# Keys of a cross-attention: one product of 128 rows per half and copies by transfers, in place of eight products of 96 rows

## What is computed

```python
x = x + xattn(layernorm(x), ctx, mask, Wq, Wk, Wv, Wo)
x = x + ffn(layernorm(x), gate_w, wi_gate, wi_up, wo)
# xattn
q = shape(H @ Wq, Lq) * dph ** (-0.5)
k = shape(T @ Wk, Lkv)
v = shape(T @ Wv, Lkv)
scores = jnp.einsum('bhqd,bhkd->bhqk', q, k) + ext      # ext: finfo.min where mask is 0
out = jnp.einsum('bhqk,bhkd->bhqd', softmax(scores), v) @ Wo
# ffn: top 2 of 8 experts for each token, a capacity for each expert and rank,
# silu(disp @ wi_gate) * (disp @ wi_up) @ wo, weighted and added back
```

## Time and profile before

| what | us |
|---|---|
| median of 3 runs (385.32 to 386.65) | 385.34 |
| the profiled execution, its own time | 385.02 |
| its span in the trace | 383.2 |
| TensorE busy, share of the span | 348.0, 91% |
| VectorE / ScalarE / GpSimd busy | 251.2 / 193.4 / 228.4 |
| last row scores of the attention's pair 14, 15 begin | 128.0 |
| first slots loaded for the experts | 170.5 |

### The profile page before, as it was taken

One profiled execution on the slowest core, in us unless ns is written; L12 is line 12 of the kernel. 1 busy time (PEld: TensorE's weight loads), 2 busy tenths in 40 slices (PEclk: granted clock), 3 DMA queues, 4 the chain that ended last, 5 costly groups with the idle time before them and its releaser, 6 DMA issues.

```text
span 383.2 us, 8985 instructions
## 1 busy us (share of the span) xinstructions
PE 348.0 (91%) x3013; PEld 304.9 (80%) x3013; DVE 251.2 (66%) x933; ACT 193.4 (50%) x439; POOL 228.4 (60%) x195
## 2 busy tenths in 40 slices
PE   5899799999999996668999999999999999999970
PEld 2566577687778764558999999999999999999970
DVE  5898999999999996604455554645546455465440
ACT  3578677787888873303344444434434343344320
POOL 6373512667667777740464573864848638368673
PEclk9899999999999998598999999999999999999995
DMA  6899301222323222124137245463373544724232
GB/s 179 244 359 297 92 7 23 63 67 67 82 55 118 72 66 68 53 60 124 15 30 168 33 42 162 37 150 54 37 173 34 114 82 38 176 21 38 28 34 21
DMA packets 41159, 34.33 MB, mean 90 GB/s; under 512 B 8337, under 2 KB 37521, under 8 KB 40977
## 3 DMA queue, kind: packets, MB, share of 16 engines
q1 hardware_dynamic: 26592, 23.67, 21.0%
q0 software_dynamic: 13568, 9.58, 18.2%
q10 hardware_dynamic: 960, 0.60, 0.6%
HBM read 21.12 MB, written 17.73 MB: 101 GB/s over the span
## 4 chain that ended last, share of the span: by engine, by line
PE 68%; DVE 14%; POOL 6%; issue 4%; ACT 3%; DMA 3%; SPq 1%; POOLq 1%; DVEq 0%; ACTq 0%
PE bank L921 18%; PE bank L676 11%; PE bank L678 10%; PE bank L677 10%; PE bank L779 5%; POOL slots L441 4%; DVE mneg L1027 4%; PE bank L747 3%; PE bank L770 2%; PE bank L912 2%; DVE rall L1077 1%; PE bank L797 1%; DMA maskr<-in_mask 1%; PE bank L730 1%; PE bank L731 1%
## 5 line engine op out<-in xcount | busy, mean ns | idle before, releaser
L475 POOL DMA_INDIRECT out<-ys,idx x80 | 125.0, 1562 | 83.8 <-DVE ys L1308 52.1
L1335 DVE TENSOR_TENSOR h<-sg,bank 128x256 f32<-128x256 f32 x160 | 66.2, 419 | 86.8 <-ACT sg L661 78.7
L661 ACT ACTIVATE sg<-bank 128x256 f32<-128x256 f32 x160 | 61.5, 385 | 107.7 <-PE bank L678 107.2
L676 PE MATMUL bank<-ex_hi,w_hi 128*128 128x256 f32 x320 | 95.8, 299 | 1.0 <-DVE ex_lo L1289 0.3
L678 PE MATMUL bank<-ex_lo,w_hi 128*128 128x256 f32 x320 | 89.5, 280 | 0.0
L677 PE MATMUL bank<-ex_hi,w_lo 128*128 128x256 f32 x320 | 89.5, 280 | 0.0
L921 PE MATMUL bank<-w_raw,h 128*128 128x128 f32 x640 | 78.0, 275 | 0.8 <-DVE h L1335 0.8
L921 PEld LDWEIGHTS bank<-w_raw,h 128*128 128x128 f32 x640 | 74.9, 192 | 0.9 <-DVE h L1335 0.9
L441 POOL DMA_INDIRECT slots<-rall,slot x64 | 62.7, 980 | 18.4 <-issue 17.5
L676 PEld LDWEIGHTS bank<-ex_hi,w_hi 128*128 128x128 f32 x320 | 60.9, 190 | 4.1 <-issue 2.5
L677 PEld LDWEIGHTS bank<-ex_hi,w_lo 128*128 128x128 f32 x320 | 61.0, 190 | 0.0
(11 more groups left out here) (122 smaller groups left out, 536.7 us busy)
## 6 DMA issues: line engine op xcount, KB each, us to landing
slots<-in_empty SPq DMA_DIRECT2D x8, 660.0 KB, 10.7
xl<-slots SPq DMA_DIRECT2D x7, 660.0 KB, 7.3
w_raw<-in_wgu SPq DMA_DIRECT2D x8, 512.0 KB, 3.7
w_raw<-in_wdn SPq DMA_DIRECT2D x8, 256.0 KB, 4.3
out<-X SPq DMA_DIRECT2D x16, 128.0 KB
X<-in_x SPq DMA_DIRECT2D x3, 512.0 KB, 5.5
out<-ys,idx POOLq DMA_INDIRECT x80, 3.3
slots<-rall,slot POOLq DMA_INDIRECT x64
```

Of the source, the lines that this page charges most:

```text
L475: nc.gpsimd.indirect_dma_start(out=out[:, :], out_offset=bass.IndirectOffsetOnAxis(ap=IDX[v][:, j:j + 1], axis=0), in_=YS[c][:, t, :], in_ ...
L661: nc.scalar.activation(SG[m % 2][:], GATE_PS[m % 2][:, 0:2 * P], ACT.Silu).then_inc(sg_ready, 1)
L676: nc.tensor.matmul(ps, hi, m_hi, start=True, stop=False)
L1335: nc.vector.tensor_tensor(H[n % 2][:, f, :], SG[m % 2][:], UP_PS[m % 2][:, 0:2 * P], ALU.mult).then_inc(h_ready, 1)
```

## The change

- `project_keys(half)`: one product of three parts with all 128 output rows for each half of the batches; the host orders Wk's columns so that output row 4c+g is feature c of group g. Half 0 is made in the front, half 1 in step 1.
- `keys_hi(half)` writes the high part over the masked context `CTXM`, `keys_lo(half)` the low part over `CTX_LO`.
- `arrange_keys(piece)` on SyncE's queue: three transfers copy hi, hi and lo into `KC`, whose layout becomes group, batch, key. Pieces are batches 0 to 1, 2 to 7 (both issued ahead of the X loads) and 8 to 15 (issued after the expert weights' loads).
- `place_keys(j)`: one transfer for each batch, 32 in place of 16 for each j.
- `mask_context(1)`, `context_hi(1)`, `context_lo(1)` move from the front into step 0.
- The mask row is formed after `context_lo(0)` and `moments(0)`.
- TensorE's front: `project_values(0)` stands before the turning of the first batch.

```diff
-PLACED = 16 * 4 * HG
+PLACED = 16 * 4 * HG * 2
-        KC = s1("kc", [P, B, GROUPS, LK])
+        KC = s1("kc", [P, GROUPS, B, LK])
-        K_PS = [MX[0], MX[1], DEN_PS, M1, M1, M1, M1, M1]
+        K_PS = M1
@@ block.sync
             for g in range(GROUPS):
-                sp.dma_start(KC[ONE_ROW:ONE_ROW + 1, :, g, :], EXT[:]).then_inc(ext_in, 16)
+                sp.dma_start(KC[ONE_ROW:ONE_ROW + 1, g, :, :], EXT[:]).then_inc(ext_in, 16)
+
+            def arrange_keys(piece):
+
+                b0, b1 = ((0, 2), (2, 8), (8, 16))[piece]
+                sp.wait_ge(k_used, b0 // 8 + 1)
+                for part in range(3):
+                    keys = CTXM[:, b0:b1, :] if part < 2 else CTX_LO[:, b0 * LK:b1 * LK].bitcast(F32)
+                    sp.dma_start(KC[32 * part:32 * part + 32, :, b0:b1, :], keys).then_inc(kc_in[piece], 16)
+
+            arrange_keys(0)
+            arrange_keys(1)
             for q in range(1, 4):
                 sp.dma_start(X[:, 8 * q:8 * q + 8, :], x_t[:, 8 * q:8 * q + 8, :]).then_inc(x_in[q + 1], 16)
...
             def place_keys(j):
-                b = slice(2 * j, 2 * j + 2)
-                to = slice(2 * j % KBUF, 2 * j % KBUF + 2)
                 done = keys_in[j % 2]
                 sp.wait_ge(st_full, 4 * (2 * j - KBUF + 2))
                 for part in range(4):
                     for h in range(HG):
                         rows = slice(32 * part + DPH * h, 32 * part + DPH * h + DPH) if part < 3 else slice(ONE_ROW, ONE_ROW + 1)
-                        sp.dma_start(KS[rows, to, :, h * LK:(h + 1) * LK].bitcast(F32), KC[rows, b, :, :]).then_inc(done, 16)
+                        for b in (2 * j, 2 * j + 1):
+                            sp.dma_start(KS[rows, b % KBUF, :, h * LK:(h + 1) * LK].bitcast(F32), KC[rows, :, b, :]).then_inc(done, 16)
...
-            sp.wait_ge(k_used, 8)
+            arrange_keys(2)
+            for piece in range(1, 3):
+                sp.wait_ge(kc_in[piece], 48)
             sp.wait_ge(ext_in, 64)
@@ block.gpsimd
-            pool.wait_ge(k_used, 4)
+            pool.wait_ge(kc_in[0], 48)
             pool.wait_ge(ext_in, 64)
             spread_keys(0)
...
                 if i + 2 < KBUF:
+                    wait(pool, kc_in[1], 48)
                     spread_keys(i + 2)
@@ block.scalar
-            def keys_hi(n):
-
-                half, g = n // 4, n % 4
-                act.wait_ge(k_full, n + 1)
-                if n == 0:
-                    act.wait_ge(kc_set, 2)
-                nc.scalar.copy(KC[0:96, 8 * half:8 * half + 8, g, :].bitcast(F32R),
-                               K_PS[n][0:96, :].rearrange("p (b k) -> p b k", k=LK)).then_inc(k_hi, 1)
+            def keys_hi(half):
+
+                act.wait_ge(k_full, half + 1)
+                nc.scalar.copy(CTXM[:, 8 * half:8 * half + 8, :].rearrange("p b k -> p (b k)").bitcast(F32R), K_PS[:]).then_inc(k_hi, 1)
@@ block.tensor
-                product3(K_PS[n][0:96, :], WK_HI[:, w], WK_LO[:, w], CTX_HI[:, cols], CTX_LO[:, cols]).then_inc(k_full, 1)
+                product3(K_PS[:], WK_HI[:], WK_LO[:], CTX_HI[:, cols], CTX_LO[:, cols]).then_inc(k_full, 1)
...
-            for n in range(4):
-                project_keys(n)
+            project_keys(0)
+            pe.wait_ge(any_ready, 1)
+            project_values(0)
...
-                if i in (0, 1):
-                    project_keys(2 * i + 4)
+                if i == 1:
+                    project_keys(1)
...
-                if i in (0, 1):
-                    project_keys(2 * i + 5)
@@ block.vector
-                lo = KC[64:96, 8 * half:8 * half + 8, g, :]
-                nc.vector.tensor_tensor(lo.bitcast(F32R), K_PS[n][64:96, :].rearrange("p (b k) -> p b k", k=LK), lo, ALU.subtract).then_inc(k_used, 1)
+                nc.vector.tensor_tensor(CTX_LO[:, 512 * half:512 * half + 512], K_PS[:],
+                                        CTXM[:, 8 * half:8 * half + 8, :].rearrange("p b k -> p (b k)"), ALU.subtract).then_inc(k_used, 1)
...
+            context_lo(0)
+            moments(0)
             dve.wait_ge(maskr_in, 16)
...
-            context_lo(0)
-            moments(0)
             keys_lo(0)
             norm(0)
             norm(1)
-            for n in range(1, 4):
-                keys_lo(n)
             queries_lo(0)
-            mask_context(1)
             moments(1)
-            context_lo(1)
             row_max(0, 0)
...
```

More of the change, by code:

```diff
@@ L138, in program @@
         ANY = s1("any", [P, B])
-        NW = GROUPS * 96
         WQ = s1("wq", [P, D])
-        WK = s1("wk", [P, NW])
-        WK_HI = s1("wk_hi", [P, NW], F32R)
-        WK_LO = s1("wk_lo", [P, NW], F32R)
+        WK = s1("wk", [P, D])
+        WK_HI = s1("wk_hi", [P, D], F32R)
+        WK_LO = s1("wk_lo", [P, D], F32R)
         SEL_HI = s1("sel_hi", [P, GROUPS, 3, 32], F32R)
@@ L223, in program @@
         k_full, k_hi, k_used = sem("k_full"), sem("k_hi"), sem("k_used")
+        kc_in = [sem(f"kc_in{v}") for v in range(3)]
         v_full, v_used = sem("v_full"), sem("v_used")
@@ L389, in _ @@
             for half in range(2):
-                nc.gpsimd.memset(KC[ONE_ROW:, 8 * half:8 * half + 8, :, :], 1.0).then_inc(kc_set, 1)
+                nc.gpsimd.memset(KC[ONE_ROW:, :, 8 * half:8 * half + 8, :], 1.0).then_inc(kc_set, 1)
             nc.gpsimd.memset(QS[1][ONE_ROW:ONE_ROW + 1, :, :].bitcast(F32), 1.0).then_inc(kc_set, 1)
@@ L408, in spread_keys @@
                     KS[0:NROW, i].rearrange("p g (h k) -> p g h k", h=HG),
-                    KC[0:NROW, i].unsqueeze(2).to_broadcast([NROW, GROUPS, HG, LK]),
+                    KC[0:NROW, :, i, :].unsqueeze(2).to_broadcast([NROW, GROUPS, HG, LK]),
                     KMASK[0:NROW].rearrange("p (g h) -> p g h", g=GROUPS).unsqueeze(3).to_broadcast([NROW, GROUPS, HG, LK]),
@@ L582, in _ @@
             ins.then_inc(sel_ready, 1)
-            for n in range(4):
-                keys_hi(n)
+            keys_hi(0)
+            keep_values(0)
             keep_turned(0)
             queries_hi(0)
-            keep_values(0)
+            keep_values(1)
             stack_queries(0, 0)
-            context_hi(1)
             stack_queries(0, 1)
-            keep_values(1)
             def step(i):
@@ L599, in step @@
                     exps(i - 1, 0)
-                if i in (0, 1):
-                    keys_hi(2 * i + 4)
+                if i == 1:
+                    keys_hi(1)
                 if there(i + 1):
@@ L618, in step @@
                     guesses(i - 1)
-                if i in (0, 1):
-                    keys_hi(2 * i + 5)
+                if i == 0:
+                    context_hi(1)
                 if there(i):
@@ L683, in keep_warm, with project_keys @@
                     nc.tensor.matmul(ST[1][:], ONES[:], ONES[:].unsqueeze(1).to_broadcast([P, 4, P]), start=True, stop=True)
-            def project_keys(n):
-                half, g = n // 4, n % 4
+            def project_keys(half):
                 pe.wait_ge(ctx_lo_ready, half + 1)
[L689 to L692, removed]
+                pe.wait_ge(wk_lo_ready, 1)
+                wait(pe, k_used, half)
                 cols = slice(512 * half, 512 * half + 512)
-                w = slice(96 * g, 96 * g + 96)
-                product3(K_PS[n][0:96, :], WK_HI[:, w], WK_LO[:, w], CTX_HI[:, cols], CTX_LO[:, cols]).then_inc(k_full, 1)
+                product3(K_PS[:], WK_HI[:], WK_LO[:], CTX_HI[:, cols], CTX_LO[:, cols]).then_inc(k_full, 1)
             def project_values(n):
@@ L843, in _ @@
             queries(0)
-            pe.wait_ge(any_ready, 1)
-            project_values(0)
             project_values(1)
@@ L980, in context_lo, with keys_lo @@
                                         CTX_HI[:, cols].bitcast(F32), ALU.subtract).then_inc(ctx_lo_ready, 1)
-            def keys_lo(n):
-                half, g = n // 4, n % 4
-                dve.wait_ge(k_hi, n + 1)
-                lo = KC[64:96, 8 * half:8 * half + 8, g, :]
-                nc.vector.tensor_tensor(lo.bitcast(F32R), K_PS[n][64:96, :].rearrange("p (b k) -> p b k", k=LK), lo, ALU.subtract).then_inc(k_used, 1)
+            def keys_lo(half):
+                dve.wait_ge(k_hi, half + 1)
+                nc.vector.tensor_tensor(CTX_LO[:, 512 * half:512 * half + 512], K_PS[:],
+                                        CTXM[:, 8 * half:8 * half + 8, :].rearrange("p b k -> p (b k)"), ALU.subtract).then_inc(k_used, 1)
             def moments(k):
@@ L1222, in step @@
                     row_max(i, 2)
-                if i in (0, 1):
-                    keys_lo(2 * i + 4)
+                if i == 0:
+                    mask_context(1)
                 if there(i):
@@ L1266, in step @@
                     added(now)
-                if i in (0, 1):
-                    keys_lo(2 * i + 5)
+                if i == 0:
+                    context_lo(1)
+                if i == 1:
+                    keys_lo(1)
                 if there(i - 1):
@@ L1364 @@
```

(5 more changed lines are left out.)

## The result

The changed kernel takes 431.4 us (median of 4 runs, 430.6 to 433.1) against 385.3 us before: 1.120 times as long, 95% interval 1.118 to 1.123. Forecast were 429 (range 406 to 435) and slower. The profiled execution took 431.9 us, its span is 430.1.

What follows compares the result with a forecast made beforehand. TensorE was taken to set the pace at 14.5 us per pair, with SyncE's queue 2 us behind as next bound. 385.0 + 42.1 (batch 14 later) + 1.7 (half clock) = 428.8, taken as 429 us; range 406 to 435.

Steps and rivals of the forecast that it cites:

- The bound: Attention: TensorE sets the pace at 14.5 us per pair of batches; SyncE's queue, at 12.6 us, is next.
- Price of an issue: place_keys on SyncE's queue: each of 32 half-size transfers still takes 0.72 us with the gap, so 23.2 us a set.
- Size hardly matters: place_keys transfers: an eighth of the bytes lowers issue time only from the median 686 ns to 619.
- The rival of cheap issues: place_keys: 0.47 us per issue, a set 15.0 us, total 383 us; chance 0.08, split into 0.04 same and 0.04 faster.
- Start of the first set: place_keys after the keys' transfers land: begins at 50.1 us instead of 39.59, behind X, fills and weights.
- the sum: Whole kernel: 385.0 us plus 42.1 for batch 14's later start plus 1.7 for half clock, 428.8 us.
- keys not held up: Rival for arrange_keys(2): its transfers don't stand in line, place_keys starts at 39.6 us, total 418 us; chance 0.17.
- The sets: place_keys: five of 23.2 us, plus 3.0 for stores between and 1.0 for landing, ending at 170.1 us.
- Lags of the others: Row scores of batches before 14: batch 6 at 74.3 us, batch 8 at 97.5, lag growing from 6 over 14 to 42.
- Front: Start up to the first row scores: comes out within a microsecond of 19.16 us.
- Clock: TensorE after stalls before batches 8 to 14: half clock, only the last counting, 1.7 us, bounds 0 and 3.5.
- What would show it: Changed profile: SyncE's queue unpaused from about 50 to 170 us, TensorE waits of 6 to 10 us named `ks<-kc`, more DMA in chain.

Runs made afterwards that it cites:

- the run of both edits: Changed kernel with 16 transfers per place_keys set and zeros and expert weights issued behind the first set: 430.4 us, 1.010 times the kernel before.
- the control: The changed kernel itself, nothing altered, run again on a chip where the kernel before takes 428.1 us: 448.2 us, ratio 1.052.

## Why the prediction was right

**The bound.** That SyncE's queue was 2 us per pair behind TensorE and would pass it is what the trace shows: no pause in it, and TensorE waiting at every even batch from 6 on and at no odd one.

**Price of an issue.** Taken 0.72 with the gap, measured 22.33 / 32 = 0.70; median 674 ns for half the bytes against 686. "Size hardly matters" held. The rival of cheap issues is out for these transfers: SyncE spent 116 us on issuing 1.0 MB (120 x 8 KB and 40 x 1 KB), which at the 312 GB/s of the earlier trace rows would be about 3 us of moving bytes, an estimate. The Trainium skill (page "DMA: Bandwidth & Descriptors", section "Issuing engines are not separate DMA queues") calls the time to initiate a transfer usually small relative to the transfer; for these copies the traces disagree.

**Start of the first set.** 50.1 forecast, 52.7 measured. The parts were off in both directions. The mask row came at 8.7 and not at 10.2, since the context was masked at 4.70 instead of 5.98. The load of Wk, the first on ScalarE's queue, is now 64 KB and not 192, which I had not considered; that this is what let the context land earlier is argued, not tested. The transfers of `arrange_keys` took 0.60 us, not 0.72. So X was issued at 15.25, not at 17.1; but then the X loads took 4.09 us to issue, where they had taken 2.39, and the last load of weights went out at 29.32, for which the forecast had 29.1. The 2.6 us come from the landing: that load landed 21.7 us after its issue, at 51.0, where the sum had 18.5 (the median of two; the last one's own was 19.0) and 47.6. The half-1 transfers landed 18.1 us after their issue. Their standing in line rested in the forecast on the 18.5 us alone; it held, and the rival "keys not held up" fell.

**The sets.** 116.2 us from 52.68 to 168.89 against 119 in the sum. With the start this makes batch 14 begin at 170.0, forecast 170.1. That the two agree to 0.1 us is luck: two errors of about 3 us cancelled.

**Lags of the others.** Batch 6 was forecast for 74.3 and came at 76.2, batch 10 for 121.7 (24.2 us after batch 8's 97.5) and came at 122.4.

**Front.** Forecast within a microsecond of 19.16, measured 17.04. The step that failed is the arrival of the context, above. It costs the forecast nothing, as it lies before the wait. That 17.04 also brought TensorE's wait of 1.54 us with it, after which nine of the ten traces of this front show half clock, the forecast did not have.

**Clock.** Forecast 1.7 us with a bound of 3.5, measured about 4.1. The mechanism was right and its size was not: I took one stretch of 3.5 us at half clock from the front, but after the wait of batch 14 it lasted about 10 us. It hit batches 6 to 12 too, where SyncE's pace hides it: on the first chip two steps between waits took 19 us instead of 14.5, so the waits were about 5 us and not the 7 to 10 I named.

**What would show it.** The waits do not name `ks<-kc`, and DMA is no larger in the chain; "issue" took its place, at 10%. A reader who looks only at the chain would miss the cause.

**Open.** That the kernel returns to 385 us with sets of 16 on a chip of the first kind was not run. For that chip the case rests on the two traces, and on the runs of the three others.

## What to carry to other kernels

Issuing is work of a queue even if no table of engines shows it: add up one iteration's issues, compare with the iteration, and ask which queue is next before a transfer is split. The small transfers of this case cost about 0.7 us of issue with 8 KB as with 16 KB, so halve their number and not their bytes; and what was issued late on the queue landed here behind all that was issued earlier on it. Gains ahead of a wait that is bound by another queue are gone, and after waits of 4.6 to 11 us TensorE came back at half clock here.

## What was not expected of the hardware

On the chips of the experiments the kernel before takes 424 to 430 us, 10 to 12% longer, with the same program. The traces there agree with the first chip's until GpSimd begins to send rows, near 68 us. After that single results of TensorE are seen late by ScalarE or VectorE, in every step or two: the waits that the profile calls "remote" are up to 3.0 us long in the run of both edits and up to 5.6 in the control, and neither trace of the result has one. In the run of both edits (430 us) the transposes of the next batch and the copy that waits for them:

```profile
104.44 0.41 PE L727 MATMUL bank<-C,xn 128*128 128x128 f32 x2
```

```profile
107.39 0.37 ACT L547 COPY xt<-bank 128x256 f32<-128x256 f32 x1 [2.67 <-remote]
```

"remote" is the profile's word for a releaser that it can't find on this core. TensorE waits with them, and its granted clock from 60 to 130 us is 0.85 where it was 1.00 (the run of both edits, then the kernel before on the first chip):

```profile
60.00:130.00 70.00, 57.40 (x474) 41.72 (x466) 49.07 (x213) 38.84 (x77) 30.98 (x33) 0.85 0.27 78
```

```profile
60.00:130.00 70.00, 68.66 (x703) 53.44 (x695) 68.72 (x323) 57.77 (x119) 45.15 (x48) 1.00 0.27 70
```

Where the delay comes from was not found, nor whether it belongs to the chip or to the time of the runs. Its consequence for this case: the same edit measures 1.12 on one chip and 1.05 on another, and the traces show why. The bound that it moves past lies at 14.5 us per pair on the one and at 20 to 24 on the other.
